# Attention layer of a graph network: ten bf16 matmuls of zeros per entry on TensorE, ahead of its transposes and sums

## The reference

```python
h = (x @ W).reshape(num_nodes, heads, C)
a_src = jnp.sum(h * att_src, axis=-1)
a_dst = jnp.sum(h * att_dst, axis=-1)
e = a_src[src] + a_dst[dst]
e = jnp.where(e > 0, e, NEG_SLOPE * e)
m = jax.ops.segment_max(e, dst, num_segments=num_nodes)
ex = jnp.exp(e - m[dst])
den = jax.ops.segment_sum(ex, dst, num_segments=num_nodes)
alpha = ex / den[dst]
msg = h[src] * alpha[:, :, None]
out = jnp.zeros((num_nodes, heads, C), h.dtype).at[dst].add(msg)
```

## Time and profile before

| | |
|---|---|
| median of 3 runs | 7895.57 us (7876.42 to 7909.71) |
| the profiled execution, its own time | 7904.27 us |
| its span, first to last instruction | 7902.4 us |
| mean granted TensorE clock over the span | 0.790 of 2.4 GHz |
| TensorE busy | 5956.0 us, 75% |
| GpSimd busy | 3831.2 us, 48% |
| VectorE busy | 4835.5 us, 61% |
| ScalarE busy | 2658.9 us, 34% |

### The profile page before, as it was taken

One profiled execution on the slowest core, in us unless ns is written; L12 is line 12 of the kernel. 1 busy time (PEld: TensorE's weight loads), 2 busy tenths in 40 slices (PEclk: granted clock), 3 DMA queues, 4 the chain that ended last, 5 costly groups with the idle time before them and its releaser, 6 DMA issues. The chain is left out here.

```text
span 7902.4 us, 163825 instructions
## 1 busy us (share of the span) xinstructions
PE 5956.0 (75%) x38014; PEld 5083.7 (64%) x38014; DVE 4835.5 (61%) x13892; ACT 2658.9 (34%) x5907; POOL 3831.2 (48%) x3975
## 2 busy tenths in 40 slices
PE   4888888888888888856767665667777676766674
PEld 4888888888888888435655553555555555555554
DVE  4666666666666666655555454556655565555557
ACT  1333333333333333212222233333333333333335
POOL 3455555545554544035555524555555555555552
PEclk7999999999999999968888776665666666666666
DMA  5444444444444444311111111111111111111111
GB/s 130 110 111 110 109 109 110 111 109 109 110 111 109 109 110 107 94 44 39 40 39 38 37 30 37 36 39 37 38 37 39 37 38 37 38 37 37 37 39 42
DMA packets 608470, 541.35 MB, mean 69 GB/s; under 512 B 307553, under 2 KB 485930, under 8 KB 608081
## 3 DMA queue, kind: packets, MB, share of 16 engines
q0 software_dynamic: 126192, 261.30, 13.9%
q1 hardware_dynamic: 356874, 163.66, 9.0%
q10 hardware_dynamic: 125272, 115.10, 5.5%
HBM read 517.22 MB, written 22.31 MB: 68 GB/s over the span
## 5 line engine op out<-in xcount | busy, mean ns | idle before, releaser
L1674 POOL DMA_INDIRECT Gt<-TAB,metat x1632 | 1586.4, 972 | 1522.5 <-DMA ad<-ADT 751.7
L520 POOL DMA_INDIRECT G<-Atab,meta x1616 | 1529.3, 946 | 1534.8 <-DVE EE L555 831.2
L659 PE MATMUL S<-oh,EE 128*128 128x64 f32 x6464 | 824.7, 280 | 218.7 <-DVE acc L586 110.8
L659 PEld LDWEIGHTS S<-oh,EE 128*128 128x128 f32 x6464 | 779.4, 196 | 283.1 <-DVE acc L586 155.6
L1166 POOL DMA_INDIRECT Gc<-XS,metac x672 | 650.0, 967 | 576.9 <-PE Sc L1336 294.5
L624 ACT COPY BS<-BK 128x512 f32<-128x512 f32 x404 | 237.0, 587 | 1861.5 <-PE BK L669 1630.5
L680 PE MATMUL S<-ohl,BS 128*128 128x64 f32 x6464 | 783.6, 274 | 6.2 <-issue 4.0
L680 PEld LDWEIGHTS S<-ohl,BS 128*128 128x128 f32 x6464 | 775.4, 195 | 13.6 <-issue 12.2
L555 DVE TENSOR_TENSOR EE<-Z,G 128x512 f32<-128x512 f32 x404 | 279.4, 692 | 783.6 <-remote 747.5
L1869 PE MATMUL SR<-P,Gt 128*128 128x128 f32 x3264 | 746.5, 400 | 0.0
L1869 PEld LDWEIGHTS SR<-P,Gt 128*128 128x128 f32 x3264 | 636.9, 291 | 114.7 <-issue 114.7
(11 more groups left out here) (269 smaller groups left out, 11712.6 us busy)
## 6 DMA issues: line engine op xcount, KB each, us to landing
mm<-MM ACTq DMA_DIRECT2D x404, 256.0 KB
ZR<-in_eft SPq DMA_DIRECT2D x404, 128.0 KB
dstb<-in_lin SPq DMA_DIRECT2D x404, 128.0 KB
Gt<-TAB,metat POOLq DMA_INDIRECT x1632
G<-Atab,meta POOLq DMA_INDIRECT x1616
ad<-ADT SPq DMA_DIRECT2D x816, 0.2 KB
WB<-Btab SPq DMA_DIRECT2D x404, 32.0 KB
Gc<-XS,metac POOLq DMA_INDIRECT x672
```

What stands on the lines that cost most here:

```text
L520: e.indirect_dma_start(G[:, k, s, :], None, Atab, bass.IndirectOffsetOnAxis(ap=meta[:, k, s:s + 1], axis=0)).then_inc(l_g[k], 16)
L659: mm = e.matmul(S1[:, a * W:(a + 1) * W], lhs, rhs, start=(s == 0), stop=(s == 3))
L1674: e.indirect_dma_start(G[:, k, s, :], None, TAB, bass.IndirectOffsetOnAxis(ap=meta[:, k, s:s + 1], axis=0)).then_inc(l_g[k], 16)
```

## The change

Two tiles of bf16 zeros are added, a weight tile `zw` of 128 x 128 and a moving tile `zm` of 128 x 512, and VectorE clears both once, ahead of its first work in the stage. TensorE's first wait is raised accordingly from 1 to 3. A helper `warm(bank, n)` issues n matmuls of the one with the other, which write zeros to a whole bank of 512 columns. It is called in `t1` (three, into `MT`), in `t4` (three, into `PT`) and in `t5` (four, into `SR`), each time behind the waits of that step and ahead of its own transposes or matmuls, which then write over the zeros. The result does not depend on them. Nothing else is changed.

```diff
+        zw = sbt(ph, "zw", [128, 128], BF16)
+        zm = sbt(ph, "zm", [128, CH], BF16)
...
         @blk.vector
         def _(e):
+            e.memset(zw[:, :], 0.0).then_inc(s_i, 1)
+            e.memset(zm[:, :], 0.0).then_inc(s_i, 1)
             e.memset(neg[:, :], -1.0).then_inc(s_i, 1)
...
         @blk.tensor
         def _(e):
-            e.wait_ge(s_i, 1)
+            e.wait_ge(s_i, 3)
             T = load_T(e, tb, 1)
+
+            def warm(bank, n):
+                for _ in range(n):
+                    e.matmul(bank[:, :], zw[:, :], zm[:, :], start=True, stop=True)
 
             def t1(j):
                 q = j.slot(2)
                 wait(e, s_m, j.at(1))
                 if not j.first(2):
                     wait(e, s_a1, j.at(-1))
+                warm(MT[q], 3)
...
                 wait(e, s_ex, j.at(1))
                 if not j.first(2):
                     wait(e, s_p, j.at(-1))
+                warm(PT[q], 3)
...
                 wait(e, s_sc, j.at(1))
                 if not j.first(2):
                     wait(e, s_u, j.at(-1))
+                warm(SR[q], 4)
```

## The result

The changed kernel takes 7701.52 us (7699.95 to 7714.37) against 7899.34 us of the kernel before on the same chip, a ratio of 0.976 (95% interval 0.973 to 0.978). It is 198 us faster. I had forecast 8212 us, slower than before.

The account below looks back on a forecast made before the run. GpSimd's gathers and TensorE's rounds, lengthened by holds, were taken to set 7.28 us an entry. Entries without a hold 81 us plus with one 236 us made 317 us on 7904: 8221 profiled, 8212 predicted, range 7790 to 8600 us.

Parts of the forecast that it names:

- three paces: Attention layer, per entry: GpSimd's gathers 5.1 us, TensorE's round 5.7 us at the low clock, 3.5 us at the high.
- holds: Attention layer: what waits for TensorE goes on only after GpSimd's four gathers, TensorE runs dry; about 139 of 408 entries.
- The price of the dummies: Ten 512-column zero matmuls per entry, priced by columns: 2.2 us at the high clock, 4.3 us at the low.
- The clock: TensorE's mean granted clock in the attention layer would rise from 0.65 to 0.8 to 0.9.
- the term of 236 us: About 139 entries with a hold: t5's four dummies cost 1.7 us each time, at the low clock after the restart.
- 81 us slower: About 269 entries without a hold: 0.3 us more each, 0.2 from longer rounds and 0.1 from rounds low altogether.
- The sign that I had named for this: PT copy's "remote" waits should stay about 139, 4 to 5 us each; fewer or shorter would make the sum wrong.
- Nothing in the change touches the gathers: Attention layer: why holds come couldn't be read from the rows, and the change leaves GpSimd's gathers alone.
- The entries without a hold: About 269 of 408: 70% stay at 5.7 us, 30% go from GpSimd's 5.1 us to 0.6 us longer; 81 us.
- The faster rival: Attention layer: high clock before the restart too, 6.8 us an entry, 195 us less, 7700 us; chance 0.17.
- the clock comes up before the restart too: Faster case's mechanism: nine tenths of TensorE's busy time at the high clock, a round of 5.95 us.
- The rule of the Trainium skill: Low clock costs half its time: 1019 us, less 898 us of dummies, gains 121 us, 7783 us; within faster's 0.17.

Follow-up runs that it names:

- e_early: Changed kernel with all ten zero matmuls ahead of the wait for the step's input, behind the wait that frees the bank: 7763.29 us, 1.007 to the kernel before.
- e_five: Changed kernel with five zero matmuls per entry (1, 2, 2) in place of ten: 7962.64 us, 1.032 to the kernel before.
- e2_five: Changed kernel with five zero matmuls per entry (1, 2, 2), on a chip without holds: 5982.62 us, 1.000 to the kernel before.
- e_tiny: Changed kernel with its ten zero matmuls cut to 16 moving columns from 512: 7766.89 us, 1.006 to the kernel before.
- e2_three_after: Changed kernel with three indirect DMAs per entry in place of four, a quarter of the edges left out: 7066.87 us, 0.917 to the kernel before.
- e_fourteen: Changed kernel with fourteen zero matmuls per entry (4, 4, 6) in place of ten: 7614.70 us, 0.989 to the kernel before.
- e_twenty: Changed kernel with twenty zero matmuls per entry (6, 6, 8) in place of ten: 7947.51 us, 1.031 to the kernel before.

## Why the prediction was wrong

**The bound.** That three paces lie below the 7.28 us, and that holds make the rest, stands. C and D show the kernel without holds: 5.13 us an entry where I had GpSimd at 5.1.

**The price of the dummies.** 0.22 us each at the high clock was right (0.216 us measured). The round with its dummies came to 5.40 us where I had added 5.7, because its real work is 3.24 us and not 3.5. The Trainium skill ("TensorE: Matmul & The Clock Gate", Back-to-back issue gap) has a sustained 131 ns for such a matmul, and the runs with ten and twenty don't agree.

**The clock.** I expected 0.8 to 0.9 and it is 0.96. The step that failed is this one: "TensorE is dry for 2.2 us or more, as now [...], and restarts at the low clock." It is dry for 1.15 us in the round shown, and the restart is at 1.00; so are 382 of 407 starts of t5. Its four dummies take 0.97 us in the median, from the first of them to the first real matmul, and not 1.7. So the term of 236 us, four dummies at the low clock in each entry with a hold, isn't there. Without it the sum would still have been 81 us slower, so this step alone doesn't turn the sign.

**The holds.** The larger mistake is that holds would come as before. I took their number and length as given by the gathers and put their change at nothing. The sign that I had named for this came: the copy's waits on "remote" are 310 of 2.7 us. The number was wrong from the start: the 139 waits with the releaser "remote" are only a part, and 246 copies were over 1 us late. And it is the holds that the change alters: those of over 4 us go from 96 to 14, and intervals over 8 us from 111 to 32 on A and from 84 to 33 on B. "Nothing in the change touches the gathers" holds for the code and not for the time: GpSimd waits for t5 to get its slots back, as I had written further down. Its waits on "remote" go from 55 to 296, and the groups that follow without a pause from 154 to 25. The sum of an entry on A is this: the dummies add 2.2 us, TensorE's idle time falls by 1.07 us (2.16 less 1.09), the real matmuls take some 1.6 us less at the higher clock, and 7.28 us become 6.80. But that is only where the time went, and not yet why: e_early has a clock of 0.90 and no gain.

**The entries without a hold.** I had added 0.3 us for each of them, TensorE's round against GpSimd's pace. On C and D it is the whole story: an entry goes from 5.13 to 5.40 us, and the kernel is 1.9% slower, the way that I had forecast for A. What it costs on A can't be told apart from the holds there.

**The faster rival.** It had 0.17 and its number, 6.8 us an entry and 7700 us, is what came: 6.80 us and 7701.5. Its condition, less than 1.3 us of an entry idle, for which I had given no working, held too (2273.70 of 2710 us busy leave 1.09 us). That the number fits to the hundredth is luck: it was made of a round of 5.95 us and a busy share of 0.873, and measured were 5.71 us busy and 0.84. Its step "the clock comes up before the restart too" is what happened, and the one that mine had wrong. But a high clock isn't enough: e_early has a clock of 0.90 and e_five 0.79, and they gain nothing or lose 3%.

The rule of the Trainium skill that I had weighed beside it (the same page, HAM oscillation), low time times one half, gives 7783 us and the right sign on A. On C an estimate by it is far off: a clock of 0.77 over 2086 us would give back 480 us, ten dummies at 0.216 us take 881, and that would be 400 us slower where 113 were measured. Neither side of that sum counts in full there, since TensorE isn't the bound before. e2_five on D is at the full clock and gains nothing, but its five dummies alone would take 441 us by the same sum, so it agrees with the rule and with this reading alike.

**What is shown and what is open.** Shown: the gain is in the intervals between entries; it needs the columns and not the instructions (e_tiny), enough of them (e_five), and behind the waits (e_early); a high clock isn't enough for it (e_early against e_tiny); without holds the change costs 1.9%; with three gathers in a group and ten dummies the holds are gone (e2_three_after). With more dummies they don't go away, they fall where TensorE doesn't run dry (e_fourteen, e_twenty).

The path that I argue for is that the dummies delay the results of t5 and t4 until they fall at a fixed place relative to the group, so that one group delays one entry and not two. Counts in the traces fit it: in the changed kernel 308 of 408 copies wait and start 1.0 to 1.6 us after the fourth gather of a group, before it were 53. But no run moves that place by itself, so the path stays argued. An obvious rival is left with it: that it takes the high clock and the delay together. Every variant with the gain has both, e_tiny has neither, and none has the delay at the low clock. Why e_five's pattern, two short and one double interval, is stable, I can't say. Open is also what differs between A, B and C, D, and why TensorE's results wait for the gathers on the first two. No variant here beats both kernels on every chip: on B ten and fourteen dummies are equal within their intervals, but on C and D ten are slower, and five, equal to none on D, are slower than none on B.

## What to carry to other kernels

- Before a wait is priced, ask whether it is a fixed amount or a phase. If engines wait for each other's groups, added work can be free, and here it was worth anything from 2.4% faster to 3.2% slower. Read the intervals between entries as a distribution, not only their mean.
- Don't count such waits by the name that the view gives their end. How late an instruction starts after its input has ended is the same measure in every run; by name the holds of e_fourteen and e_twenty looked gone.
- A gain that comes from a wait which ends with no visible releaser should be measured on more than one chip. This one is 0.976, 0.988, 1.019 and 1.019 on A to D, and the kernel before itself takes 7899, 7708, 5977 and 5981 us.
- The dummy matmuls lifted the clock; five of them did it fully on a chip without holds. That gained nothing where GpSimd was the bound (e2_five), and where TensorE was the bound each cost its 0.216 us.

## What the runs showed of the hardware that was not expected

- The same program takes 5977 us on one chip and 7899 us on another, 32% more, and on each of the two it repeats within 0.5%. The difference lies in the three stages with indirect DMAs and not between them; in the first layer TensorE is busy for 2000.00 of 2000 us on C and for 1751.14 on A.
- On A it isn't TensorE's results alone: of 8126 sequencer instructions of SyncE in the attention layer (DMA issues left out), 1225 take over 0.4 us, all but 2 of them while GpSimd gathers or within 1.3 us behind. On C none does.
- On A, in the changed kernel, of the 323 copies that wait and start over 1 us late, 308 start 1.0 to 1.6 us after the fourth gather of a group has ended (1.36 us in the round shown). In the kernel before it is less regular, 53 of 184, and 76 of them start inside a group. Every instruction with a wait on "remote" in the layer is one that takes TensorE's results: the copies of PT and NL, the new maximum, the sums and the gathers.
- A busy TensorE doesn't end this by itself: with twenty dummies it is busy for 2210.00 of 2210 us, and the maximum still waits in 381 of 408 entries. With ten dummies and three gathers the holds are gone on B, and an entry takes 5.40 us, to the hundredth as on D.
- The clock was at the high level throughout with TensorE busy for 86% of the time on D (e2_five), and at 0.77 for the same share on C in the kernel before:

```profile
3900.00:5600.00 1700.00, 1459.85 (x9110) 1034.69 (x9274) 1404.97 (x4639) 913.00 (x2319) 1296.37 (x1325) 1.00 0.28 53
```
